# Cluster sums from three exact bf16 parts of x, and one matmul for the channel sum of squares, in a fused clustering and 1x1 convolution kernel

## The reference

```
sim = einsum('bchw,nc->bnhw', xn, cn); idx = argmax(sim, axis=1)
onehot = one_hot(idx, N)
sum_x = einsum('bhwn,bchw->bnc', onehot, x); count = sum(onehot)
gathered = (sum_x / max(count, 1))[b, idx]
delta = gathered - x
alpha = exp(-mean(delta * delta, channels))
y = x + alpha * delta
out = relu(einsum('oc,bchw->bohw', W, y) + b)
```

## Time and profile before

| | |
|---|---|
| median of 3 runs | 431.25 us |
| profiled execution: its own time | 431.4 us |
| its span | 429.6 us |
| PE busy | 422.2 us, 98% |
| DVE / ACT / POOL busy | 285.3 / 243.4 / 206.7 us |
| granted TensorE clock | full throughout |

### The profile page before, as it was taken

The page is one execution under the profiler, slowest core; times in us unless marked ns, Lnnn a source line. Parts: engine busy times, 40 slices in busy tenths (PEclk is TensorE's granted clock), DMA queues, the critical chain, the costliest instruction groups (busy, mean ns, idle before and its releaser), DMA issues.

```text
span 429.6 us, 5789 instructions
## 1 busy us (share of the span) xinstructions
PE 422.2 (98%) x2134; PEld 296.0 (69%) x2134; DVE 285.3 (66%) x378; ACT 243.4 (57%) x329; POOL 206.7 (48%) x102
## 2 busy tenths in 40 slices
PE   8999999999999999999999999999999999999996
PEld 6744466775777667775867757776677758777785
DVE  2368979485776767495883857767674956787730
ACT  5665385566465673565754664656735657555541
POOL 2000665486284482674553862844826745424330
PEclk9999999999999999999999999999999999999999
DMA  8996298976577946859379665879463220222123
GB/s 275 309 291 122 56 261 219 274 218 166 143 244 185 226 168 164 215 149 256 99 198 265 169 175 142 242 182 229 163 170 125 98 99 0 98 99 98 49 112 134
DMA packets 70927, 73.94 MB, mean 172 GB/s; under 512 B 2724, under 2 KB 45732, under 8 KB 70900
## 3 DMA queue, kind: packets, MB, share of 16 engines
q1 hardware_dynamic: 70900, 73.58, 61.9%
HBM read 48.40 MB, written 25.17 MB: 171 GB/s over the span
## 4 chain that ended last, share of the span: by engine, by line
PE 95%; DVE 2%; ACT 1%; issue 1%; POOL 0%; POOLq 0%; DVEq 0%
PE main L797 20%; PE main L799 20%; PE main L798 20%; PE sump L740 10%; PE fa L700 9%; PE gat L771 5%; PE al L778 1%; PE fa L709 1%; PE al L779 1%; PE al L819 1%; PE fa L724 1%; PE main L840 1%; PE al L785 1%; PE gat L785 1%; PE gat L812 1%
## 5 line engine op out<-in xcount | busy, mean ns | idle before, releaser
L284 POOL TENSOR_TENSOR z<-z,x 128x1024 f32<-128x1024 f32 x42 | 99.3, 2384 | 147.1 <-DVE z L389 147.1
L797 PE MATMUL main<-yh,wh 128*128 128x512 f32 x376 | 152.5, 406 | 0.0
L799 PE MATMUL main<-yh,wl 128*128 128x512 f32 x376 | 147.0, 391 | 0.0
L798 PE MATMUL main<-yl,wh 128*128 128x512 f32 x376 | 146.7, 390 | 0.0
L291 POOL TENSOR_TENSOR yl<-z,yh 128x1024 fp32r<-128x1024 f32 x44 | 106.0, 2423 | 57.9 <-ACT yh L530 57.9
L369 DVE TENSOR_TENSOR z<-gat,x 128x1024 f32<-128x1024 f32 x46 | 56.2, 1221 | 91.1 <-PE gat L771 91.1
L538 ACT ACTIVATE o<-main,bcol 128x512 f32<-128x512 f32 x96 | 65.7, 686 | 82.8 <-PE main L799 82.8
L797 PEld LDWEIGHTS main<-yh,wh 128*128 128x128 f32 x376 | 70.7, 188 | 20.4 <-issue 4.6
L799 PEld LDWEIGHTS main<-yh,wl 128*128 128x128 f32 x376 | 70.6, 188 | 15.2
L798 PEld LDWEIGHTS main<-yl,wh 128*128 128x128 f32 x376 | 70.7, 188 | 14.3
L530 ACT ACTIVATE yh<-z 128x1024 fp32r<-128x1024 f32 x48 | 50.5, 1052 | 22.9 <-POOL z L284 21.9
(11 more groups left out here) (114 smaller groups left out, 325.5 us busy)
## 6 DMA issues: line engine op xcount, KB each, us to landing
x<-x SPq DMA_DIRECT2D x24, 1024.0 KB, 5.7
out<-o SPq DMA_DIRECT2D x23, 1024.0 KB, 4.8
xs<-x SPq DMA_DIRECT2D x84, 256.0 KB, 6.3
o<-w SPq DMA_DIRECT2D x1, 1024.0 KB, 12.3
out<-o SPq DMA_DIRECT2D x4, 256.0 KB, 2.1
sq<-centroids SPq DMA_DIRECT2D x2, 80.0 KB
bcol<-bias SPq DMA_DIRECT2D x1, 2.0 KB, 11.7
```

The source lines that it names most:

```text
L284: pool.tensor_tensor(z, z, X[g // PARTS % 2][:, pair(h), span(g)], ALU.add).then_inc(y_pool, 1)
L797: t_.matmul(main[:, o % 2, :], WH[:, k, rows], YH[g % 2][:, k, :], start=(k == 0), stop=False)
L798: t_.matmul(main[:, o % 2, :], WH[:, k, rows], YL[g % 2][:, k, :], start=False, stop=False)
L799: last = t_.matmul(main[:, o % 2, :], WL[:, k, rows], YH[g % 2][:, k, :], start=False, stop=(k == KC - 1))
```

## The change

Four things, of which the first two are the main ones.

- **Cluster sums in bf16.** From unit 6 on (`split`), x transposed is cut exactly in three bf16 numbers: the upper half word of the f32, the upper half word of the rest, and the rest of that. `first_rest` on POOL makes `XR = XT - upper(XT)` over 2048 elements; `second_rest` on DVE writes `XR - upper(XR)` over 2048 elements as bf16 in the lower half words of `XR`. PE then does three bf16 matmuls where it did one in f32. `first_rest(g + 5)` is put at the end of POOL's turn; `second_rest(g + 3)` at the end of DVE's first and second slots, and in the third slot between `delta(g, 0)` and `scale(g - 1, 0)`.
- **One matmul for the sum of squares.** ACT copies the upper 64 partitions of `al` down (`move_upper`), DVE adds them to the lower 64 (`fold`), the two fp32r parts share one 128-partition tile `SHL`, and one matmul with ones sums both.
- **Order.** In the third slot the one-hots are transposed first, then one group of the convolution, then the sums, then the second gather. `sum_squares` goes behind the last group of the convolution, `exp(g)` to the next turn behind the last relu. The argmax is cut in `best_sims` and `first_best`; the second half of the second slot's transpose goes behind it.
- 9 warming matmul calls at the start become 6; `rank` shares the buffer `part`; the DMA scratch is made smaller to hold `XR`.

```diff
+def split(g):
+    return g >= 2 * PARTS and g % PARTS < SPLIT
...
+            def first_rest(g):
+
+                pool.wait_ge(tr_done, g - PARTS + 1)
+                xt = XT[:, g % PARTS, :, :]
+                pool.tensor_tensor(XR[:, g % PARTS, :, :].rearrange("p t c -> p (t c)"),
+                                   xt.rearrange("p t c -> p (t c)"), halfword(xt, 1), ALU.subtract
+                                   ).then_inc(rest1_done, 1)
+
             for g in range(UNITS):
                 y_half(g, 0)
                 y_half(g, 1)
                 low_half(g, 0)
                 low_half(g, 1)
+                if g + 5 < UNITS and split(g + 5):
+                    first_rest(g + 5)
...
+            def second_rest(g):
+                dve.wait_ge(rest1_done, splits(g))
+                xr = XR[:, g % PARTS, :, :]
+                v_.tensor_tensor(halfword(xr, 0), xr.rearrange("p t c -> p (t c)"), halfword(xr, 1), ALU.subtract
+                                 ).then_inc(rest2_done, 1)
...
+            def fold(g):
+                dve.wait_ge(upper_done, folded(g))
+                v_.tensor_tensor(al[0:LOW, :], upper_sum[:, :], al[0:LOW, :], ALU.add).then_inc(fold_done, 1)
...
+            def move_upper(g):
+                act.wait_ge(s_done, folded(g))
+                a_.activation(upper_sum[:, :], al[LOW:P, :], ACT.Copy).then_inc(upper_done, 1)
...
                 square(g, 0)
                 if beside and p == 2:
+                    evacuate_onehot(b + 1)
+                    relu(g - 2, 0)
                     high_half(g - 1, 0)
                     copy_sums(b + 1)
-                    evacuate_onehot(b + 1)
                     square(g, 1)
                     high_half(g - 1, 1)
-                    means(b + 1)
-                    relu(g - 2, 0)
+                    scale_means(b + 1)
+                    move_upper(g)
+                    high_means(b + 1)
                     high_sum(g)
                     relu(g - 2, 1)
...
+                if split(PARTS * b + u):
+
+                    pe.wait_ge(oh3_done, b + 1)
+                    pe.wait_ge(rest2_done, splits(PARTS * b + u))
+                    for t in range(HALF):
+                        for i, x_part in enumerate((halfword(XT[:, u, :, :], 1), halfword(XR[:, u, :, :], 1),
+                                                    halfword(XR[:, u, :, :], 0))):
+                            for h in range(2):
+                                tile = HALF * h + t
+                                last = t_.matmul(sumP[NPAD * h:NPAD * (h + 1), :], oh3[:, slot(u, tile), 0:NPAD],
+                                                 x_part[:, tile * C:(tile + 1) * C],
+                                                 start=(u == 0 and t == 0 and i == 0),
+                                                 stop=(u == PARTS - 1 and t == HALF - 1 and i == 2))
...
-                t_.matmul(al[:, :], ones[:, :], SH[:, :], start=True, stop=False)
-                t_.matmul(al[:, :], ones[:, :], SL[:, :], start=False, stop=True).then_inc(one_done, 1)
+                t_.matmul(al[:, :], ones[:, :], SHL[:, :], start=True, stop=True).then_inc(one_done, 1)
```

More of the change, by code:

```diff
@@ L57, in made, with splits @@
     return by_vector, 2 * g + h + 1 - by_vector
+def split(g):
+    return g >= 2 * PARTS and g % PARTS < SPLIT
+def splits(g):
+    return sum(split(i) for i in range(g + 1))
 def folded(g):
@@ L180, in squares, with halfword @@
             return SQ[:, :, :] if h == 0 else gat[:, :, :]
+        def halfword(words, which):
+            return words.rearrange("p t c -> p (t c)").bitcast(BF16).rearrange("p (c w) -> p c w", w=2)[:, :, which]
         def plain(b):
@@ L431, in _ @@
             keep_transposed()
-            argmax(0)
+            best_sims(0)
+            first_best(0)
             for k in range(KC):
@@ L444, in _ @@
                 delta(g, 1)
-            argmax(1)
+            best_sims(1)
+            first_best(1)
             scale(0, 0)
@@ L461, in _ @@
             rest_of_mean(1)
+            parts_of_mean(1)
+            fold(2)
             low_sum(2)
-            parts_of_mean(1)
             transpose_half(6, 0)
@@ L469, in _ @@
                 delta(g, 0)
+                if beside and p == 2 and split(g + 3):
+                    second_rest(g + 3)
                 scale(g - 1, 0)
@@ L479, in _ @@
                 add_squares(g)
-                if beside and p < 2:
+                if beside and p == 0:
                     transpose_half(g + 4, 1)
+                fold(g)
                 if beside and p == 2:
                     rest_of_mean(b + 1)
+                if beside and p == 1:
+                    best_sims(b + 1)
                 low_half(g - 1, 1)
@@ L486, in _ @@
                 if beside and p == 1:
-                    argmax(b + 1)
+                    first_best(b + 1)
+                    transpose_half(g + 4, 1)
                 if beside and p == 2:
@@ L492, in _ @@
                         transpose_half(g + 4, 1)
+                if g + 3 < UNITS and split(g + 3) and p < 2:
+                    second_rest(g + 3)
             g = UNITS - 1
@@ L607, in _ @@
             evacuate_onehot(0)
-            means(0)
+            scale_means(0)
+            high_means(0)
             act.wait_ge(b_in, 16)
@@ L628, in _ @@
             square(2, 1)
-            means(1)
+            scale_means(1)
+            high_means(1)
+            move_upper(2)
             high_half(1, 1)
@@ L660, in _ @@
                         relu(g - 2, 1)
+                    move_upper(g)
+                    high_half(g - 1, 1)
                     high_sum(g)
-                    high_half(g - 1, 1)
                     if beside:
@@ L918, in _ @@
                 convolve(g - LAG, 2)
-                if beside:
-                    sum_squares(g)
                 convolve(g - LAG, 3)
-                if not beside:
-                    sum_squares(g)
+                sum_squares(g)
             for g in range(UNITS - LAG, UNITS):
```

54 lines of the change are left out of this document (33 added, 21 removed).

## The result

The changed kernel takes **454.05 us** (median of 4 runs, 453.71 to 454.92) against 431.63 of the kernel before (4 runs, 431.1 to 432.27): ratio 1.052, 95% interval 1.0503 to 1.0536. It is 22.4 us slower.

A forecast was written before the change was run, and what follows sets the result against it. PE, with a matmul in flight for 98% of the span, bounds the kernel. Six images at 6.05 us make 36.3, less 0.9 outside: 431.4 + 35.4 = 466.8, prediction 467 us, range 438 to 486.

The forecast's parts named there:

- added work alone: Rival: DVE and POOL do not exclude each other, PE waits 3.7 us per image, 441 us; chance 0.18 including cases in between.
- PE's work, -1.95 per image: PE in the loop: bf16 sums save 1.25 us per image, one sum-of-squares matmul less saves 0.23 three times.
- What the others gain: Added instructions: second_rest 2.26 us and fold 0.65 on DVE, move_upper 0.60 on ACT, first_rest 4.75 on POOL.
- The exclusion: DVE and POOL instructions with two SBUF operands cannot overlap: first_rest and second_rest exclude each other, second_rest excludes y_half and low_half.
- First slot, no wait: First slot of an image, 15.9 us: first_rest and second_rest take turns on the port, PE waits for none of it.
- Second slot, 1.4: Second slot: y_half three microseconds late, relu of chunk 1 ends at 13.3, PE waits 1.4 us before chunk 3.
- Third slot, 2.8 + 1.3 + 1.8 + 0.65: Third slot: PE waits for the third unit's sums, add_halves, the chunk 1 relu and late one-hots; together 6.6 us.
- The sum: Per image 6.6 + 1.4 - 1.95 = 6.05 us, 36.3 for six images; sums of squares outside give 0.9 back.
- outside the images only sums of squares change: Outside the six images: four sums of squares (unit 2 and the last three) give 0.9 us back.

The follow-up runs named there:

- e1: Changed kernel with DVE's second_rest replaced by an in-place transpose of the same 2048 elements, reading one SBUF operand; 439.43 us, ratio 1.0181.
- e13: e12 with f32 sums for all units, so no first_rest or second_rest, all else the same; 429.86 us, 0.9961 of the kernel before.
- e4: Changed kernel with second_rest behind both scale instructions in the third slot, not ahead of them; 467.54 us, ratio 1.0831.
- e3: Changed kernel with only the first two of an image's three units split, the third with f32 sums; 435.22 us, ratio 1.0085.
- e2: Changed kernel with no unit split: f32 sums, no rests, new order and merged sum of squares kept; 439.85 us, ratio 1.0187.
- e11: e2 with PE and ACT in the third slot in the order of the kernel before; 434.64 us, ratio 1.0073.
- e12: e3 with second gather ahead of the sums, unit 6's transposes behind the loop's first delta, and three order changes on ACT and DVE; 432.35 us, ratio 1.0016.
- e5: Changed kernel with first_rest subtracting the f32 tile from itself instead of its upper half words; 454.68 us, ratio 1.0534.
- e6: Changed kernel, all units split, with the relu of chunk 1 ahead of high_sum (third slot: ahead of scale_means); 455.95 us, ratio 1.0563.
- e9: e3 with PE's second gather ahead of the sums in the third slot; 433.2 us, ratio 1.0045.

## Why the prediction was right, and where it was not

The direction, the mechanism and the range held (454.05 in 438 to 486; 467 was forecast). The number alone says little: 454 lies 13 us below the forecast and 13 above the 441 of "added work alone". What decides between the two is e1 and the lengthened instructions, not the time. By the prediction's own steps:

- **PE's work, -1.95 per image.** The 36 sums took 4.1 us (2.74 for 24, from 210.77, and 1.4 for 12, from 215.58) for a forecast of 4.05: bf16 runs in two column tiles at the assumed 0.113 us, and the merged sum of squares gave its 0.23. But e13, which has no waits in the steady images, loses 0.39 of a period where three times 0.23 were due: the new order costs PE some 0.3 us per image. By the starts of PE's instructions, 0.1 of it lies between the second gather and what follows it (0.54 against 0.44 before) and 0.1 between the sums and the convolution behind them (the first two matmuls are 0.33 apart, not 0.23). I had this at nothing.
- **What the others gain.** `fold` 0.68 and `move_upper` 0.60 as said; `second_rest` 2.51 to 2.62 alone, not 2.26. **The term that was mis-sized is `first_rest`**: 3.60, not 4.75. I had both bounds (3.6 and 4.75) and reasoned from 2.4 ns an element that little could be fixed; half of the 1024-element instruction is. The Trainium skill (GPSIMD Engine Reference, Performance versus the Vector engine) has 4497 ns for a tensor_tensor of that size in f32; the trace's 3.60 is 0.9 below it. No run had a `first_rest` of 4.75, so whether the rest of the schedule would then have come out as forecast is not shown.
- **The exclusion.** Shown by e1, at some 13 of its 14.6 us. It holds both ways and for half-word operands, so "the added work alone" (441) falls as a forecast; e1 is that rival made real, and measured 439.43. The Trainium skill's rule (SBUF — State Buffer, "SBUF: two separate sides") of a whole instruction held by whoever starts first agrees with every pair above, e4's 0.06 us included.
- **First slot, no wait.** Right for the steady images.
- **Second slot, 1.4.** Wrong: none. With 3.60, `y_half` there starts at 195.63, 3.9 into the slot, instead of 6.1. `first_rest` was lengthened by the port to 5.96, so the exclusion did reach this slot, but within the slack.
- **Third slot, 2.8 + 1.3 + 1.8 + 0.65.** The three places are right, to the instruction and the releaser; the sizes are 1.91, 1.01 and 1.25, and the one-hots' 0.65 is absent. The idle sum is 4.17. Against e13's slot with 1.25 less work (17.70) the slot is 4.93 longer, so each wait costs a quarter of a microsecond beyond the idle time that the trace lists. The starts show where: ahead of chunk 3 they are 1.63 us apart (224.53 to 226.16) where 0.23 is usual, which is 1.40 lost for 1.25 listed, and the next start comes after 0.34 instead of 0.23.
- **The sum.** Forecast 6.6 + 1.4 - 1.95 = 6.05 per image. Measured 4.93 - 1.95 + 0.3 = 3.3. Times six: 36.3 against 19.8.
- **Missed altogether: +3.9 in the first slot of the loop.** I wrote that outside the images only sums of squares change. There relu(0,2) and the relu of chunk 1 stand behind a `high_sum` that is late by `move_upper` and `fold`, and unit 2's sum of squares and `exp` moved into the slot; which weighs how much is open. The slot is 20.3 us with the split of three, two or no units (the changed kernel, e3, e2 and e11); the bf16 parts have no share in it. Two errors, +16.5 and -3.9, partly cancelled, and that part of the forecast's nearness is luck.

Of the whole 22.4 us, then: the third unit's split costs 18.8, the order of the third slot 4.9 and the rest of the change (`move_upper`, `fold`, the places outside the third slot) 3.2, while the other two units' split gains 4.6. These shares hold for removing the parts in this sequence and no other: in the order of e12 and e13 the same split of two units costs 2.5 us.

## What to carry to other kernels

Shortening the busiest engine's work pays only if what makes it shorter is ready in time: 7.5 us of PE work were bought with a chain POOL, DVE, POOL, ACT that passed one shared port twice. Where two engines that share a port are to do one pass each on the same data, count each pass as if both engines did it, and see whether one of them can do with a single SBUF operand (in e1 such an instruction held nobody up). Put work that other engines wait for (the second gather) ahead of work that only has to be done (the sums), and the relu that frees a buffer ahead of anything that isn't due: the order alone moved the kernel with f32 sums by 10 us with the same instructions (e2, e13).

## What the runs showed of the hardware

- POOL's subtraction of 2048 f32 elements per partition takes 3.60 us and one of 1024 takes 2.38: by a straight line through these two sizes some 1.2 us are fixed, an estimate. On DVE, where 2048 take 2.51 to 2.62 and 1024 take 1.22, no such part shows. A half-word second operand changes nothing on POOL (e5). On DVE `second_rest`, with its half-word output, took 0.25 more than the f32 rows of 512 and 1024 elements give when drawn on to 2048 (2.26).
- The port passes from one engine to the other between two back-to-back instructions of the holder: DVE, waiting since 187.50, got it at 189.75, though POOL's next instruction was in its queue. POOL's list does not keep it. In e4 it went to and fro in the same way, starting with POOL, which was 0.06 us ahead.
- With each of e4's six pauses of PE of 3.97 to 4.03 us the granted clock fell to the level of 1.2 GHz. Pauses of 1.82 to 1.91 us left it in full in the changed kernel and in e6. But in e9's profiled execution it fell 1.2 us after a pause of 1.76, which other executions had at full clock: a pause of this size costs the clock in some executions and not in others.
- A wait of PE costs about 0.25 us more than its listed idle time: matmuls that last 0.39 start 0.23 apart while they follow each other, and that overlap is lost at a pause.
